# Expert stages whose list rows carry their token and weights, with six shared groups ahead of the list and list places of 256 and 128 rows

## The chip, the cores and the metric

The kernel runs on one core of one Trainium2 chip. The metric is the device time of one launch in microseconds (us). Three runs of the kernel before took 3293.65, 3300.22 and 3301.5 us, so the median is 3300.22. A separate execution was taken with the hardware profiler. It took 3303.56 us, and its span, from the first instruction to the last, is 3301.8 us. Every row shown below comes from that one execution. A profile names the engines PE (TensorE matmul), PEld (TensorE's weight load, which overlaps PE), DVE (VectorE), ACT (ScalarE), POOL (GpSimd) and SP (SyncE, whose queue issues most DMAs).

## The reference

The input `x` is 32 sequences of 128 tokens with 256 features, 4096 tokens in all. Six blocks are added to it one after another: a state space model, a cross attention, a transformer block with gated experts, a recurrence, a second cross attention, and a second expert block. The change touches the two expert blocks. The first of them, cut to what matters:

```
logits = h2 @ router_w                       # (4096, 8)
probs = softmax(logits); topw, topi = top_k(probs, 2); topw = softmax(topw)
combine = sum(one_hot(topi, 8) * topw[..., None], axis=1)
shared = (silu(h2 @ sh_gate) * (h2 @ sh_up)) @ sh_down
gate = einsum('td,edf->etf', h2, e_gate)
up = einsum('td,edf->etf', h2, e_up)
eout = einsum('etf,efd->etd', silu(gate) * up, e_down)
spec = einsum('etd,te->td', eout, combine)
return X + shared + spec
```

The width of an expert is 512. The second expert block has sigmoid scores, one up projection, no gate and no shared part. All arithmetic is in 32-bit floats.

## The kernel before

Tokens are worked on in 8 groups of 512 (`NG = 8`, `GT = 512`; a group is 4 tiles of 128 tokens, one per partition). The program is a run of stages. Each stage writes one instruction list per engine, by hand, in the order in which the functions are called, and engines meet at semaphores. No planner sets the order in the expert stages. At the end of a stage every engine drains and waits for the others (`pass_stage`, L2564). The stages `mamba`, `b`, `c` come ahead, then `d` (`experts`, from L1902), `r` with `e` behind it, and last `f` (`list_experts`, from L2412).

Stage `d` has four parts.

1. Each group's rows `H` are transposed and the router's logits are computed (L1693, L1978). Then VectorE alone picks the two experts of every token and gives each of the 8192 pairs of a token and an expert a row in a list in DRAM, sorted by expert (`router_vector`). The list is cut into places of 256 rows (`UR`), each of one expert. The number of rows per expert is known only on the chip, so 39 places are always worked on (`units_of_list`), whatever the counts are. In the end each place's expert is looked up (`expert_i`).
2. Four *shared* units (`SHN = NG // 2`), one per group: gate and up matmuls with 512 columns (L2229), silu on ScalarE (L2250), the product on VectorE (L2262), the down matmuls (L2187) and the add to `X` (L2279). Beside them VectorE copies a group's rows to a staging buffer (`stage_group`, L2093), and GpSimd sends them to the list with 64 indirect DMAs (L2118). There are two staging buffers. VectorE's copy for the next group waits until the DMAs of the buffer's last group have landed.
3. Thirty-nine *list* units. SP loads a place's rows (L2311) and its expert's weights into one of two buffers (L2318: gate and up, 1 MB, L2321: down, 0.5 MB). PE transposes the rows of the next place during a unit (L2214) and ScalarE copies them out of PSUM (L2239). The down matmuls of a unit are issued behind the next unit's first quarter (`f == 0`). VectorE copies their result to `y_rows` (L2281), and SP stores it to `out_by_expert` (L2325).
4. The other four shared units. GpSimd gathers, for each group, 8 tiles from `out_by_expert` (L2141). It has two buffers too. VectorE multiplies them by the pair's weights and adds them to `X` (`collect_group`, L2155), in pairs of groups between the products of the units.

Within a unit the quarter `f` on PE may start when the product of quarter `f - 2` is done (`after(pe, hidden, ...)`).

Stage `f` works on its own list in DRAM, `rows_in_place`, with a fixed region of 4096 rows per expert. It was filled during stage `e` with rows of 272 floats: 256 features, 8 weights and the token's number 8 times. Each of its 39 units loads a place (L2444) and weights into three buffers (L2447). VectorE reads weights and tokens out of the rows, scales the result (L2516), and GpSimd adds each tile of 128 rows to `out` in DRAM, by token, with an indirect DMA that accumulates (L2525). Two such DMAs may not overlap in the rows that they change, so GpSimd waits for a place's DMAs to land before it issues the next place's:

```
pl.wait_ge(mixed, UT * u + UT)
pl.wait_ge(sent_to, u + 1)
after(pl, added, 16 * UT * u)
```

The results `y` have two buffers. The table of places of stage `f` is computed by VectorE at the end of stage `e` (`ended_vector`, L848 to L863).

## Time and profile before

| what | value |
|---|---|
| time of the profiled execution, its span | 3303.56 us, 3301.8 us |
| median of three runs | 3300.22 us |
| busy share of the span | PE 84%, PEld 57%, DVE 58%, ACT 46%, POOL 44% |
| stage `d` from its first DMA to the next stage's first | 1409.56 to 2108.61 us |
| stage `f` from its first matmul to the end of the span | 2997.00 to 3301.8 us |
| HBM traffic | 154.17 MB read, 90.05 MB written, 74 GB/s over the span |

The page says which engines are busy overall. It mixes stages with different limits, so for a change in two stages a reader needs the same numbers for stretches of those stages, and then the instructions in order of time. "Idle before", in square brackets behind an instruction, is how long its engine did nothing just before it and what ended that. PE's clock in a stretch is the granted share of full speed. "x16" behind a row is the number of records it merges. Each float32 matmul of this program shows as two records, and a transpose as one.

### The profile page before, as it was taken

What the parts mean: (1) busy time and instruction counts of PE and PEld (TensorE: products, weight loads), DVE (VectorE), ACT (ScalarE), POOL (GpSimd) and SP (SyncE); (2) the same over time, 40 slices, a digit from 0 to 9 for tenths busy, and PEclk for the clock granted to TensorE, in tenths of its full rate; (3) what the DMA queues carried; (4) which work ended last, traced back from release to release, by engine and by line L of the source; (5) the groups of instructions that cost most, each with busy time, mean ns of one, the idle gap of its engine ahead of it and who ended that gap; (6) DMA issues with size and microseconds to landing.
All of it is one profiled execution on the core that took longest, in us unless ns stands there. A gap on an engine that the chain in (4) does not pass through costs nothing.

```text
span 3301.8 us, 49294 instructions
## 1 busy us (share of the span) xinstructions
PE 2775.8 (84%) x16680; PEld 1894.1 (57%) x16680; DVE 1904.4 (58%) x3429; ACT 1529.9 (46%) x2627; POOL 1460.3 (44%) x1559
## 2 busy tenths in 40 slices
PE   6888888867887888776999998699788888867998
PEld 2333333334555566533888885498455555546887
DVE  3878788875887688841222223500689888862111
ACT  4565556635675566510222221344566666642222
POOL 3666676654444577525000004500345555543444
PEclk8999999998998899988999999799899999988999
DMA  9600000000013000012566652200000100005775
GB/s 326 214 1 0 0 1 0 1 0 30 14 47 110 1 1 1 1 69 92 175 192 196 196 188 82 86 1 1 1 14 31 38 30 31 21 27 175 212 211 149
DMA packets 135984, 244.92 MB, mean 74 GB/s; under 512 B 16144, under 2 KB 107792, under 8 KB 125328
## 3 DMA queue, kind: packets, MB, share of 16 engines
q1 hardware_dynamic: 115344, 208.33, 19.4%
q0 software_dynamic: 20448, 34.11, 4.2%
q8 instruction: 110, 1.80, 0.2%
q14 instruction: 82, 0.67, 0.1%
HBM read 154.17 MB, written 90.05 MB: 74 GB/s over the span
## 4 chain that ended last, share of the span: by engine, by line
PE 34%; POOL 7%; DVE 6%; issue 6%; ACT 2%; POOLq 1%; another core or an unknown queue 1%; DMA 0%; SPq 0%; DVEq 0%; ACTq 0%
PE PS L2229 9%; PE PS L2187 5%; PE PS L1837 4%; PE PS L2476 4%; PE PS L2463 4%; POOL e_hs L1396 2%; POOL rows_by_expert L2118 2%; DVE e_mx L1299 1%; POOL e_qs L1399 1%; PE PS L1251 1%; POOL rows_in_place L831 1%; PE PS L1828 1%; PE PS L1194 1%; POOLq L2564 1%
## 5 line engine op out<-in xcount | busy, mean ns | idle before, releaser
L534 POOL TENSOR_TENSOR u_in<-dtx,b_rep 128x512 f32<-128x512 f32 x256 | 324.9, 1291 | 209.1 <-ACT b_rep L515 208.0
L550 DVE TENSOR_TENSOR_SCAN state<-PS,u_in 128x512 f32<-128x512 f32 x256 | 312.2, 1219 | 59.1 <-POOL u_in L534 34.9
L2250 ACT ACTIVATE d_act_b<-PS 128x256 f32<-128x256 f32 (+1 forms) x188 | 78.4, 419 | 511.7 <-PE PS L2229 432.7
L507 PE MATMUL PS<-scaled,ident 128*128 128x512 f32 x512 | 290.6, 651 | 28.6 <-DVE scaled L544 28.6
L2229 PE MATMUL PS<-d_unit_T,d_w 128*128 128x256 f32 x1248 | 284.0, 381 | 1.0 <-ACT d_unit_T L2239 1.0
L2262 DVE TENSOR_TENSOR d_hid<-d_act_b,PS 128x256 f32<-128x256 f32 (+1 forms) x188 | 87.3, 466 | 316.9 <-ACT d_act_b L2250 314.1
L1396 POOL TENSOR_TENSOR e_hs<-e_pr 128x512 f32<-128x512 f32 x128 | 162.6, 1270 | 229.3 <-ACT e_pr L1363 225.5
L2229 PEld LDWEIGHTS PS<-d_unit_T,d_w 128*128 128x128 f32 x1248 | 235.2, 191 | 32.0 <-issue 1.4
L523 ACT ACTIVATE PS<-dt,decay_rate 128x508 f32<-128x508 f32 x256 | 173.5, 686 | 132.0 <-DVE state L550 130.2
L544 DVE TENSOR_TENSOR scaled<-state,PS 128x512 f32<-128x512 f32 x256 | 169.4, 664 | 63.9 <-PE PS L488 52.2
L2136 POOL COPY d_slot_now<-d_slot 128x8 int32 x8 | 1.5, 194 | 461.1 <-DMA out_by_expert<-d_y_rows 443.3
L2525 POOL DMA_INDIRECT out<-f_y,f_token x78 | 121.1, 1553 | 185.0 <-DVE f_token L2509 117.8
L2187 PE MATMUL PS<-d_w,d_hid 128*128 128x256 f32 x880 | 198.0, 379 | 1.5 <-DVE d_hid L2262 1.5
L2187 PEld LDWEIGHTS PS<-d_w,d_hid 128*128 128x128 f32 x880 | 167.5, 190 | 28.2 <-issue 3.4
L1299 DVE TENSOR_REDUCE e_mx<-PS 128x8 f32<-128x1024 f32 x128 | 155.7, 1217 | 41.4 <-PE PS L1242 41.4
L1359 ACT ACTIVATE e_pT<-PS 128x1024 f32<-128x1024 f32 x128 | 130.7, 1021 | 96.2 <-PE PS L1251 96.2
L2516 DVE TENSOR_SCALAR f_y<-PS,f_share_rows 128x256 f32<-128x256 f32 x78 | 37.7, 483 | 235.1 <-PE PS L2463 220.8
L1251 PE MATMUL PS<-ident,e_pr 128*128 128x128 f32 x1024 | 144.7, 287 | 25.7 <-ACT e_pr L1363 25.3
L507 PEld LDWEIGHTS PS<-scaled,ident 128*128 128x128 f32 x512 | 96.4, 203 | 118.0 <-DVE scaled L544 86.0
L1837 PE MATMUL PS<-r_ring,r_wh 128*128 128x128 f32 x1024 | 161.3, 290 | 0.0
L1303 DVE TENSOR_TENSOR e_pr<-PS,e_mx 128x1024 f32<-128x1024 f32 x128 | 156.7, 1224 | 4.4
L1251 PEld LDWEIGHTS PS<-ident,e_pr 128*128 128x128 f32 x1024 | 122.0, 148 | 62.9 <-ACT e_pr L1363 55.0
(426 smaller groups left out, 6411.6 us busy)
## 6 DMA issues: line engine op xcount, KB each, us to landing
d_w<-in_d_w SPq DMA_DIRECT2D x41, 1024.0 KB, 4.9
f_w<-in_f_w SPq DMA_DIRECT2D x39, 1024.0 KB
rows_in_place<-blank SPq DMA_DIRECT2D x136, 272.0 KB, 4.5
d_w<-in_d_w SPq DMA_DIRECT2D x41, 512.0 KB, 3.9
f_unit_rows<-rows_in_place SPq DMA_DIRECT2D x39, 272.0 KB, 5.1
rows_by_expert<-zeros SPq DMA_DIRECT2D x39, 256.0 KB, 2.8
d_unit_rows<-rows_by_expert SPq DMA_DIRECT2D x39, 256.0 KB, 4.0
out_by_expert<-d_y_rows SPq DMA_DIRECT2D x39, 256.0 KB, 4.0
```

Source lines behind the costliest of these rows:

```text
L507: nc.tensor.matmul(YB[:, c], ident[:], scaled[:, (KD * n + c) % RC], start=False, stop=n == NS - 1).then_inc(m_y, 1)
L523: nc.scalar.activation(seqs(DECAY[:, k % RD])[:, :, 1:L], seqs(dt[:, p, c])[:, :, 1:L], ACT.Exp, scale=decay_rate[:, c * NS + n:c * NS + n ...
L534: nc.gpsimd.tensor_tensor(u_in[:, k % RU], dtx[:, p, c], b_rep[:, n % RB], ALU.mult).then_inc(m_u, 1)
L544: nc.vector.tensor_tensor(scaled[:, k % RC], state[:, k % 2], CB, ALU.mult).then_inc(m_hc, 1)
L550: nc.vector.tensor_tensor_scan(state[:, k % 2], DECAY[:, k % RD], u_in[:, k % RU], 0.0, ALU.mult, ALU.add).then_inc(m_h, 1)
L1251: step = nc.tensor.transpose(TR[:, m], pr[:, i % 2, m], ident[:])
L1299: nc.vector.tensor_reduce(mx[:, i % 2], scores_of(i), AX.X, ALU.max).then_inc(maxed, 1)
L1303: nc.vector.tensor_tensor(pr[:, i % 2], scores_of(i), mx[:, i % 2].unsqueeze(2).broadcast_to([128, MAPS, L]), ALU.subtract).then_inc(shift ...
L1396: nc.gpsimd.tensor_tensor(hs[:, i % 2], pr[:, i % 2, :, 0:L // 2], pr[:, i % 2, :, L // 2:L], ALU.add).then_inc(halved, 1)
L1837: product = nc.tensor.matmul(bank(at, m), wh_k[:, k, m * 128:m * 128 + 128], wide(ring[:, k, (at - 1) % (2 * WIN)]), start=False, stop=k = ...
L2187: step = nc.tensor.matmul(out_h[:, q], hid[:, p, f, row:row + 128], w_down[:, r, f], start=f == 0, stop=f == FC - 1)
L2229: step = nc.tensor.matmul(b, wt[:, r, c, f * 128:f * 128 + 128], x, start=c == 0, stop=c == KD - 1)
```

## The change

Stage `d` takes over what stage `f` does. The rows in `H` get 16 more floats: 8 with the token's weight for each expert and 8 with its number. They go to the list straight from `H`, with no staging copy. Unit results are scaled by VectorE and added by GpSimd, place by place, to a table by token in DRAM (`out_by_token`, zeroed in stage `b`). At the end SP loads that table in 8 pieces into four buffers, and VectorE adds it to `X`. Six shared units stand ahead of the list and two behind it.

Both expert stages get places of two sizes. There are 31 of 256 rows and 9 of 128 rows (71 tiles of 128 rows, where 39 places of 256 have 78). In stage `d` the order is one large place, nine times large, large, small, large, and three large ones. In stage `f` a small place stands behind every third or fourth large one. An expert's rows fill large places, and its last rows a small one where they fit. The tables are computed on VectorE with more and wider operations.

```
+def split_units(groups):
+    halves = (2 * groups * GT - 8) // 128 + 8
+    single = 8 + halves % 2
+    return (halves - single) // 2, single
+def unit_plan(groups):
+    full, single = split_units(groups)
+    kinds, done = [], 0
+    for n in range(full):
+        kinds.append((2, 2 * n))
+        if (n + 1) * single // full > done:
+            kinds.append((1, 2 * full + done))
+            done += 1
+    return kinds
+def slot_order(groups):
+    full, single = split_units(groups)
+    order = [(2, 0)]
+    for n in range(single):
+        order += [(2, 3 * n + 1), (2, 3 * n + 2), (1, n), (2, 3 * n + 3)]
+    return order + [(2, n) for n in range(3 * single + 1, full)]
+def half_of(groups):
+    full = split_units(groups)[0]
+    return [2 * n if kind == 2 else 2 * full + n for kind, n in slot_order(groups)]
...
-        SHN = NG // 2 if gated else 0
+        SHN = NG - 2
...
-            share_t = share.rearrange("p g s j -> p (g s) j")
-            for j in range(2):
-                link(V.tensor_copy(share_t[:, :, j], top[:, j]))
+            link(V.tensor_tensor(top[:, 4], top[:, 3], top[:, 2], ALU.subtract))
+            dve.sem_inc(routed, 1)
+            dve.wait_ge(exped, 2)
+            link(V.tensor_scalar(top[:, 0], top[:, 4], 1.0, None, ALU.add))
+            link(V.reciprocal(top[:, 0], top[:, 0]))
+            link(V.tensor_tensor(top[:, 1], top[:, 4], top[:, 0], ALU.mult))
+            link(V.tensor_tensor(lg[:], best[:, 0], by_e(top[:, 0]), ALU.mult))
+            link(V.tensor_tensor(tmp[:], best[:, 1], by_e(top[:, 1]), ALU.mult))
+            dve.wait_ge(marked, 2)
+            link(V.tensor_tensor(src_wide.rearrange("p g k d -> p (g k) d")[:, :, D:D + E], lg[:], tmp[:], ALU.add))
...
+            twice, single = units_e[:, E:], units_e[:, 0:E]
+            link(V.tensor_copy(count[:, 0], until[:, :, TILES - 1]))
+            link(V.tensor_scalar(count[:, 1], until[:, :, TILES - 1], -128.0, None, ALU.add))
+            link(V.tensor_tensor(filled[:], count.rearrange("p z e -> p (z e)").unsqueeze(2).broadcast_to([128, 2 * E, FILLS]),
+                                 whole.unsqueeze(1).broadcast_to([128, 2 * E, FILLS]), ALU.is_gt))
             link(V.tensor_reduce(units_e[:], filled[:], AX.X, ALU.add))
-            link(V.tensor_tensor_scan(last_e[:], ones_e[:], units_e[:], 0.0, ALU.mult, ALU.add))
-            link(V.tensor_tensor(base_e[:], last_e[:], units_e[:], ALU.subtract))
-            link(V.tensor_scalar(base_e[:], base_e[:], float(UR), None, ALU.mult))
+            link(V.tensor_tensor(starts[:, 1:E + 1], single, twice, ALU.subtract))
+            link(V.tensor_scalar(twice, twice, 2.0, None, ALU.mult))
+            link(V.tensor_tensor_scan(ends[:, 0:E], ones_e[:, 0:E], twice, 0.0, ALU.mult, ALU.add))
+            link(V.tensor_scalar(starts[:, 0:1], ends[:, E - 1:E], float(2 * FULL), None, ALU.max))
+            link(V.tensor_tensor_scan(ends[:, E:], ones_e[:], starts[:], 0.0, ALU.mult, ALU.add))
+            link(V.tensor_tensor(base_e[:, 0], ends[:, 0:E], twice, ALU.subtract))
+            link(V.scalar_tensor_tensor(out=base_e[:, 1], in0=ends[:, E + 1:], scalar=-1.0, in1=ends[:, 0:E], op0=ALU.add, op1=ALU.subtract))
+            link(V.tensor_copy(base_e[:, 2], twice))
+            link(V.tensor_scalar(base_e[:], base_e[:], 128.0, None, ALU.mult))
...
+            link(V.tensor_tensor(moved[:], place[:], over_n(2), ALU.is_ge))
+            link(V.tensor_tensor(moved[:], moved[:], over_n(1), ALU.mult))
+            link(V.tensor_tensor(place[:], place[:], over_n(0), ALU.add))
+            link(V.tensor_tensor(place[:], place[:], moved[:], ALU.add))
...
-        def stage_group(dve, turn, p):
-            g = 2 * turn + p
-            after(dve, in_list[p], 16 * 2 * GS * turn)
-            nc.vector.tensor_copy(staged_rows[:, p], rows_full[:, g])
-            nc.vector.tensor_copy(slot_now[:, p], slot[:, g]).then_inc(staged, 1)
...
         def to_list_pool(pl):
-            pl.wait_ge(listed, 16 * UNITS)
-            def group(turn, p):
...
+            for g in range(NG):
                 for k in range(GS):
                     for j in range(2):
                         nc.gpsimd.indirect_dma_start(
...
+                            rows_by_expert, bass.IndirectOffsetOnAxis(slot[:, g, k, j:j + 1], 0),
+                            src_wide[:, g, k], None).then_inc(in_list[g % 2], 16)
+        def to_tokens_pool(pl):
+            done = 0
+            for j in range(UNITS):
+                pl.wait_ge(taken, 2 * (j + SHN) + 4)
+                for k in range(tiles_at[j]):
+                    nc.gpsimd.indirect_dma_start(
+                        out_by_token, bass.IndirectOffsetOnAxis(token[:, j % 2, k:k + 1], 0), y_rows[:, j % 2, k], None,
+                        bounds_check=NG * GT - 1, oob_is_err=False, compute_op=ALU.add).then_inc(added, 16)
+                done += tiles_at[j]
+                pl.wait_ge(added, 16 * done)
+                pl.sem_inc(scattered, 1)
+        def note_vector(dve, j, jp, kind):
+            n = tiles_of[kind]
+            if isinstance(j, int):
+                dve.wait_ge(row_in[jp], 16 * (j // 2 + 1))
             else:
...
+                dve.wait_ge(row_in[jp], 8 * (j - jp) + 16)
+            nc.vector.tensor_tensor(mine_rows[:, jp, 0:n], unit_rows[:, jp, 0:n, D:D + E],
+                                    mine[:, j].unsqueeze(1).broadcast_to([128, n, E]), ALU.mult).then_inc(weighed, 1)
+            dve.wait_ge(scattered, j + 1)
+            nc.vector.tensor_copy(token[:, jp, 0:n], unit_rows[:, jp, 0:n, D + E]).then_inc(noted, 1)
+            dve.wait_ge(weighed, 2 * j + 1)
+            nc.vector.tensor_reduce(share_rows[:, jp, 0:n], mine_rows[:, jp, 0:n], AX.X, ALU.add).then_inc(weighed, 1)
+        def collect_group(dve, g):
+            dve.wait_ge(taken, 2 * (g + 2 + (UNITS if g >= SHN else 0)))
+            dve.wait_ge(got[g % GOT], 16 * (g // GOT + 1))
+            nc.vector.tensor_tensor(X[:, g], X[:, g], y_got[:, g % GOT], ALU.add).then_inc(combined, 1)
...
-                    step = nc.vector.tensor_copy(y_rows[:, p, h:h + 1], o)
-                step.then_inc(taken, 1)
+                    step = nc.vector.tensor_scalar(y_rows[:, p, h], o[:, 0], share_rows[:, p, h:h + 1], None, ALU.mult)
...
+            with eng.Fori(0, SINGLE) as turn:
+                j = 4 * turn + 1
                 unit(eng, j + SHN, *LST(j, 1), LST(j - 1, 0), "list")
-                unit(eng, j + (SHN + 1), *LST(j + 1, 0), LST(j, 1), "list")
-            unit(eng, SHN + UNITS - 2, *LST(UNITS - 2, 1), LST(UNITS - 3, 0), "list")
-            unit(eng, SHN + UNITS - 1, *LST(UNITS - 1, 0), LST(UNITS - 2, 1), None)
-            before = LST(UNITS - 1, 0)
-            for g in range(SHN, NG if SHN else 0):
-                now = SHR(g, 1 - g % 2)
-                unit(eng, UNITS + g, *now, before, None, again=g - SHN)
-                before = now
-            output(eng, (UNITS + NG if SHN else UNITS) - 1, *before)
-        def load_rows(sp, j, jp):
+                unit(eng, j + (SHN + 1), *LST(j + 1, 0), LST(j, 1), "half")
+                unit(eng, j + (SHN + 2), *LST(j + 2, 1, "half"), LST(j + 1, 0), "list")
+                unit(eng, j + (SHN + 3), *LST(j + 3, 0), LST(j + 2, 1, "half"), "list")
...
+        def load_rows(sp, j, jp, at, tiles):
             after(sp, turned, j - 1)
-            sp.dma_start(unit_rows[:, jp], list_units[:, j]).then_inc(row_in[jp], 16)
+            after(sp, weighed, 2 * j - 3)
+            after(sp, noted, j - 1)
+            sp.dma_start(unit_rows[:, jp, 0:tiles], list_rows[:, bass.ds(at, tiles)]).then_inc(row_in[jp], 16)
...
+            sp.wait_ge(scattered, UNITS + 2)
+            for g in range(NG):
+                after(sp, combined, g - GOT + 1)
+                sp.dma_start(y_got[:, g % GOT], out_rows[:, g]).then_inc(got[g % GOT], 16)
...
-        unit_of = rows_in_place.rearrange("(u r p) d -> p u r d", p=128, r=UT)
+        rows_at = rows_in_place.rearrange("(h p) d -> p h d", p=128)
+        tiles = [n for n, _ in unit_plan(NG)]
+        upto = [sum(tiles[:u]) for u in range(SLOTS + 1)]
+        late = lambda u: upto[max(u, 0)]
+        wide = lambda u: tiles[u] * 128```

GpSimd's instructions of stage `d` in their order before (`d_slot_now` is a copy of a group's list positions; the first DMAs scatter rows to the list, the last gather results):

```order
L2115 TENSOR_TENSOR d_mark<-eps 128x1
L2118 DMA rows_by_expert<-d_staged_rows,d_slot_now 9984x256 x8
...
L2136 COPY d_slot_now<-d_slot 128x8
L2138 TENSOR_TENSOR d_mark<-eps 128x1
L2141 DMA d_big<-out_by_expert,d_slot_now 128x256 x8
```

and now, the whole of the stage:

```order
L2425 MEMSET d_unit_no 128x1 x40
L2154 COPY H<-d_tokens 128x32x8
L2164 DMA rows_by_expert<-H,d_slot 9216x272 x64
L2173 DMA out_by_token<-d_y_rows,d_token 4096x256 x71
```

The scatters lost the waits between groups. The gathers are gone, and 71 DMAs that accumulate now run during the list.

PE in the loop over the list, one unit before (`d_unit_T` holds the place's rows, transposed):

```order
L2229 MATMUL PS<-d_unit_T,d_w 128x256 x4
...
L2187 MATMUL PS<-d_w,d_hid 128x256 x4
...
L2187 MATMUL PS<-d_w,d_hid 128x256 x4
L2229 MATMUL PS<-d_unit_T,d_w 128x256 x4
...
L2214 MATMUL PS<-ident,d_unit_rows 128x128 x4
```

and now the small unit of a turn, with the start of the large unit behind it:

```order
L2253 MATMUL PS<-d_unit_T,d_w 128x128 x4
...
L2209 MATMUL PS<-d_w,d_hid 128x256 x4
...
L2209 MATMUL PS<-d_w,d_hid 128x256 x4
L2253 MATMUL PS<-d_unit_T,d_w 128x128 x4
...
L2238 MATMUL PS<-ident,d_unit_rows 128x128 x4
...
L2253 MATMUL PS<-d_unit_T,d_w 128x256 x4
...
L2209 MATMUL PS<-d_w,d_hid 128x256 x4
L2253 MATMUL PS<-d_unit_T,d_w 128x256 x4
```

The small unit's own matmuls have half the columns, but the 8 down matmuls of the large place ahead of it stand inside it. Its own 4 stand in the large unit behind it.

VectorE at the seam between two list units, before:

```order
L2262 TENSOR_TENSOR d_hid<-d_act_b,PS 128x256
L2274 ISA
L2276 ISA
L2281 COPY d_y_rows<-PS 128x256
L2276 REGISTER_ALU
L2281 COPY d_y_rows<-PS 128x256
```

and now, from the last product of a unit to the first of the next (`d_token` holds a place's token numbers as integers):

```order
L2279 TENSOR_TENSOR d_hid<-d_act_b,PS 128x256
...
L2186 TENSOR_TENSOR d_mine_rows<-d_unit_rows,d_mine 128x16
L2188 REGISTER_ALU
L2189 CAST d_token<-d_unit_rows 128x2
L2190 ISA
L2191 TENSOR_REDUCE d_share_rows<-d_mine_rows 128x2
L31 ISA
L2278 ISA
L2279 TENSOR_TENSOR d_hid<-d_act_b,PS 128x256
```

Three instructions (`note_vector`) came in between. The cast waits until GpSimd's DMAs of the place two before have landed, and the next unit's first product is queued behind it.

## Rows read from the trace of the kernel before

**Rows 1.** Stretches: us, then busy us and records per engine, PE clock, DMA share, GB/s.

```profile
1451.00:1564.00 113.00, 84.55 (x230) 45.37 (x229) 27.41 (x58) 10.17 (x18) 63.96 (x72) 0.86 0.28 99
1564.00:1985.00 421.00, 421.00 (x2017) 370.43 (x2018) 97.56 (x230) 90.45 (x229) 0.00 (x0) 1.00 0.59 189
1985.00:2108.00 123.00, 95.59 (x297) 56.87 (x295) 46.03 (x102) 10.48 (x19) 64.62 (x80) 0.93 0.27 77
3000.00:3290.00 290.00, 288.46 (x1403) 252.17 (x1403) 51.64 (x194) 86.72 (x235) 118.02 (x76) 1.00 0.73 207
```

**Rows 2.** Chain that ended last: start us, length us, what; both lists.

```profile
1563.85 3.75 PE PS L2229 x8
...
1965.66 5.18 PE PS L2229 x24
...
1976.46 5.18 PE PS L2229 x24
...
3271.31 2.59 PE PS L2476 x12
...
3278.66 2.59 PE PS L2476 x12
```

**Rows 3.** Timeline, end of the list: start us, length us, engine, line, operation [idle before].

```profile
1974.34 0.42 DVE L2281 COPY d_y_rows<-PS 128x256 f32<-128x256 f32 x1 [1.23 <-PE PS L2187]
...
1980.02 0.38 ACT L2250 ACTIVATE d_act_b<-PS 128x256 f32<-128x256 f32 x1 [1.34 <-PE PS L2229]
1980.43 0.42 DVE L2262 TENSOR_TENSOR d_hid<-d_act_b,PS 128x256 f32<-128x256 f32 x1 [1.31 <-ACT d_act_b L2250]
...
1990.11 3.60 PE L2229 MATMUL PS<-d_xT,d_w 128*128 128x512 f32 x8
...
1997.00 13.90 PE L2229 MATMUL PS<-d_xT,d_w 128*128 128x512 f32 x32
```

**Rows 4.** Timeline of weight loads in the recurrence.

```profile
2161.17 0.30 PEld L1828 LDWEIGHTS PS<-r_xT,r_wi 128*128 128x128 f32 x2
2161.39 1.17 PEld L1837 LDWEIGHTS PS<-r_ring,r_wh 128*128 128x128 f32 x8
2162.48 0.30 PEld L1828 LDWEIGHTS PS<-r_xT,r_wi 128*128 128x128 f32 x2
```

**Rows 5.** Timeline, the router's end and the first product of the shared units.

```profile
1453.35 0.17 DVE L2064 TENSOR_TENSOR d_base_e<-d_last_e,d_units_e 128x8 f32<-128x8 f32 x1
...
1454.66 0.42 DVE L2068 TENSOR_TENSOR d_place<-d_place,d_base_e 128x256 f32<-128x256 f32 x1
...
1457.54 0.48 DVE L2074 TENSOR_TENSOR d_passed_e<-d_const,d_last_e 128x312 f32<-128x312 f32 x1
...
1459.79 0.68 DVE L2262 TENSOR_TENSOR d_hid<-d_act_b,PS 128x512 f32<-128x512 f32 x1
```

**Rows 6.** Timeline, the last group collected and the stage's end.

```profile
2104.46 3.38 DVE L2155 SCALAR_TENSOR_TENSOR X<-d_big,d_share_now,X 128x256 f32<-128x256 f32 x8 [4.99 <-DMA d_big<-out_by_expert,d_slot_now]
2108.61 0.35 SPq L1757 DMA_DIRECT2D r_wi<-in_r_wi  x1
```

**Rows 7.** Waits in stage f: engine, for whom: us in total, times, longest.

```profile
POOL out L2525 <- DVE f_token L2509: 117.8, 27, 24.2
POOL out L2525 <- DMA out<-f_y,f_token: 47.3, 10, 5.0
```

**Rows 8.** Timeline of stage f, a result on VectorE and the DMAs on GpSimd.

```profile
3059.33 1.55 POOL L2525 DMA_INDIRECT out<-f_y,f_token  x1 [4.96 <-DMA out<-f_y,f_token]
3061.18 1.55 POOL L2525 DMA_INDIRECT out<-f_y,f_token  x1 [0.30 <-issue]
3065.84 1.55 POOL L2525 DMA_INDIRECT out<-f_y,f_token  x1 [3.11 <-DVE f_token L2509]
...
3270.05 0.48 DVE L2516 TENSOR_SCALAR f_y<-PS,f_share_rows 128x256 f32<-128x256 f32 x1 [1.14 <-PE PS L2463]
...
3271.31 1.55 POOL L2525 DMA_INDIRECT out<-f_y,f_token  x1 [3.85 <-DVE f_token L2509]
```

517 lines of the change are left out of this document (241 added, 276 removed).

## The prediction

> **What bounds the kernel now.** I read the stretches first. Through the list of stage `d` PE is busy 421.00 of 421.00 us at the full clock, 2.4 GHz; in stage `f` it is busy 288.46 of 290. The four shared units ahead of the list keep it busy for only 84.55 of 113 us, the four behind it for 95.59 of 123 [rows 1]. So both lists cost what PE's instructions cost, and around the first list something else sets the time. The chain gives the unit: large places of `d` follow each other by 10.80 us, those of `f` by 7.35, and 24 records of 256 columns take 5.18 us, 0.216 each [rows 2]. A place of `d` is 48 such records (10.35 us) and 4 transposes (the other 0.45); one of `f` is 32 records (6.9) and 4 transposes. A record of 512 columns takes 13.90 / 32 = 0.43 us [rows 3].
>
> **Stage `d`, ahead of the list.** The router's chain on VectorE grows, and the first product waits behind it. A step costs 0.17 us at 8 elements, 0.42 at 256 and 0.48 at 312 [rows 5], so about 1 ns per element more, and 0.04 between steps. Added: three wide steps for the weights less two copies (+1.1), eight small ones and two widened for the counts (+1.8), three wide ones for the positions (+1.4), the wider table of places (+1.7, with two steps of 680 elements at 0.9). A staging copy less is -0.7, three small steps behind one tiny matmul at the stage's start about +0.5. Sum +5.8: the first product moves from 1459.79 to 1465.6 us and PE goes on at 1466.3. Then come 6 x 32 - 16 = 176 records of 512 columns (75.5 us) and 160 down records (34.5), and 2 us for a slower clock behind the gap (the granted mean of that stretch is 0.86 [rows 1]). That is 1578.4; 2.1 us of transposing and copying the first place, an estimate from its 4 transposes and two ScalarE copies, puts the first list matmul at 1580.5 instead of 1563.85 [rows 2]: **+16.7**. Two shared units of 20.6 us are in this. They are cheap because PE idled there: the scatters keep GpSimd busy for 64 of 113 us [rows 1] and have no staging to wait for now. They hide behind 112 us of PE.
>
> **The list.** Before: 1563.85 to 1990.11 [rows 2, 3], 426.3 us. After: 31 x 10.80 + 9 x 5.40 = 383.4, plus the down records of the last shared unit (6.9) less its own last ones (3.45): 386.9, so -39.4. This takes a small place at half price, which no row shows. From below: a load of the weights is hidden behind 256 columns now, and the nearest stream of small matmuls, the recurrence, starts loads 0.11 us apart (2161.17 to 2161.39, two loads), with ScalarE's waits 1.31 / 10 = 0.131 [rows 4]. Half price is 0.108. I take 0.115, the nearest row being 0.11: 288 records x 0.007 = +2.0. The upper end is 0.131 (+6.6), and if load and matmul did not overlap at all 0.214 (+30).
>
> The Trainium skill weighs against half price ("TensorE: Matmul & The Clock Gate", section "Back-to-back issue gap"): in a stream of loads and matmuls both set the spacing, and at 128 columns it gives 81 ns where a matmul alone is 56. By its 25 ns more per record this term would be 7.2 us instead of 2.0. The recurrence's 0.131 agrees with it, its 0.11 does not.
>
> Silu and product of a large place's last quarter end 0.94 us behind its matmuls (0.38 and 0.42 with hand-offs, 1980.02 to 1980.85 [rows 3]); a small place's quarter covers 0.86. With a hand-off to PE that is 0.15 nine times: +1.4.
>
> **The new wait.** VectorE may write a place's tokens only when GpSimd's DMAs of the place two before have landed, and the next product is queued behind it; PE waits for that product at its third quarter. No row of `d` shows such a landing, but stage `f` has the same DMAs. Call L the time from the end of the last issue to the next place's issue. Landing ended it 10 times, 47.3 us, longest 5.0 [rows 7], as 4.96 at 3059.33; three times of four VectorE ended it, so that L was shorter, 3.11 at 3065.84 [rows 8]. The mean over all is at most 7.35 - 3.4 = 3.95. An issue takes 1.55 and 0.30 between two, so 3.40 for a large place, and GpSimd starts 0.78 behind the result (3270.53 to 3271.31) [rows 8].
>
> Behind a small unit the room is least. It starts; 0.86 + 3.45 later the large place ahead is out, +0.5 for VectorE [rows 3], +0.8, +3.4, +L; the unit lasts 7.35; cast, reduction and product take 0.8. The product is there 2.45 + L into the large unit, and PE wants it at 5.64 (three quarters and transposes): a stall of L - 3.2, nine times. Between large units there is room up to L = 7.4. With L = 3.8: 9 x 0.6 = **+5.4** (L of 3.2: 0; of 5.0: +16). I take 3.8 because the mean was at most 3.95 and DMA gets busier by the ninth that the list gets shorter. List: -39.4 + 2.0 + 1.4 + 5.4 = **-30.6**.
>
> **Behind the list.** Before: 1990.11 to 2108.61 [rows 3, 6], 118.5 us, with waits of PE for products queued behind collecting; at the end VectorE waits 4.99 us for a gather [rows 6]. After: 64 records of 512 columns (27.5), 80 down records (17.25), the last add to `X` (1.7), two adds of 1024 elements (1.2 each by the rate above), 0.8 to the next stage: 49.7. The loads from the table can start 15 us in (3.4 + 3.5 + 0.5 + 0.8 + 3.4 + 3.8) and are wanted at 31, so they hide. **-68.8**. Stage `d` in all: 16.7 - 30.6 - 68.8 = **-82.7**.
>
> **Stage `f`.** PE's part falls from 39 x 7.35 = 286.7 to 35.5 x 7.35 = 260.9, -25.7. But a turn of three large and one small place is 25.7 us on PE and 3 x 3.40 + 1.55 + 4L = 11.75 + 4L on GpSimd. They meet at L = 3.5. With 3.8 GpSimd sets the pace: 1.2 us more, nine times, +10.8. PE's own small extras (1.0 and 1.4) hide under that. At the end the last, small place waits for the large one's landing: its issue comes 4.2 later, less 1.85 for the issue that is gone, +2.4. **-12.5** (L of 3.2: -21; of 5.0: +35). The longer table at the end of stage `e` (8 us instead of 5) runs beside its last scatters, and the other edits are small memsets on idle GpSimd: nothing.
>
> **Sum.** -82.7 - 12.5 = -95.2. Against the profiled execution, 3303.56, that is 3208.4. The median is 3.3 below it, so on its scale **3205 us**. For L above 3.9 the change as a whole is 50L - 286.
>
> **Rivals.**
> 1. *GpSimd keeps up* (L at most 3.5). For it: 3.11 at 3065.84, and 27 of the waits ended on VectorE [rows 7, 8]. Against: DMA share is 0.73 already [rows 1]. Stage `d` -86, `f` -22: 3192.
> 2. *Landing under load* (L of 4.3 to 5.7). For it: 4.96 happens now, with DMA at 0.73 [rows 1, 8]. Against: it happens once in four. With 5.0: -36, 3264.
> 3. *Slower than before*: the same wait with L over 5.7, from where 50L - 286 is positive. The small places then make GpSimd the limit of all of `f` and stall every turn of `d`. At 6.0: 3314. Against it: the longest wait now is 5.0 [rows 7], and the traffic grows by a ninth.
> 4. *Small places not at half price*: with 0.131 3210, with 0.214 about 3237. Against: the loads 0.11 apart [rows 4].
>
> The Trainium skill has a rule for the second and third ("DMA: Bandwidth & Descriptors", section "Latency and other measured facts"): access to HBM takes 0.2 us on average and 2 at high load. By it a landing of 3.1 could become 4.9, and the sum -41; the trace agrees that both lengths occur, 3.11 and 4.96.
>
> **How the numbers follow.** Forecast, L of 3.5 to 4.3: 0.55, by itself 3190 to 3230. Rival 1: 0.22. Rival 2: 0.12. Rival 3: 0.04. Rival 4 by more than 10 us: 0.07. Eight in ten lie between 3186 and 3245: below are only the fastest cases of rival 1, above are rival 3 and most of 2. A measurement of this kernel tells 0.3%, 10 us, from no change. Faster by more is all but rival 3 and the worst of rival 2: 0.95; within 0.3%: 0.01; slower: 0.04.
>
> **What would show it.** First list matmul near 1580 us; periods of 10.8 with 5.4 for a small unit; no wait of PE for products except one in four large units, below 1.5 us; 50 us from the last list matmul to the next stage; a turn of `f` of 26 to 27.5 us with GpSimd waiting for its own DMAs most of the time. The prediction is wrong if 128 columns cost over 0.13 us, if PE waits for weights in the lists, or if a place of `f` takes over 7.6 us.

## The result: slower by 1.2%, where 2.9% less was forecast

Before: 3300.86 us median of 4 runs (3293.65 to 3305.23). After: 3342.61 us median of 4 runs (3327.26 to 3345.07). The ratio is 1.0121, with a 95% interval of 1.0102 to 1.0140. The forecast was 3205 us, range 3186 to 3245: wrong, on the other side of no change. In the profiled executions the span goes from 3301.8 to 3342.3 us. Placed like the forecast's steps:

| stretch | before, us | after, us | forecast | measured | missed by |
|---|---|---|---|---|---|
| up to the first list matmul of `d` | 1563.85 | 1640.64 | +16.7 | +76.8 | 60.1 |
| list of `d` | 426.3 | 429.5 | -30.6 | +3.2 | 33.8 |
| behind the list, to the next stage | 118.5 | 49.8 | -68.8 | -68.8 | 0 |
| the rest, nearly all of it stage `f` | 1193.2 | 1222.5 | -12.5 | +29.3 | 41.8 |
| sum | | | -95.2 | +40.5 | 135.7 |

Later sessions ran on chips where the kernel before takes 3270 us and the one after about as much. That is a finding (below), and it explains most of the first row.

### The profile page after: what moved, and what is told of

Its sections match the earlier page's. It is cut to its first block, busy times and chain, and to the rows that moved or that the text cites. A ratio compares the mean times of both kernels' runs of the same rounds, so it can differ in the third digit from the quotient of the medians.

```text
span 3342.3 us, 49458 instructions
## 1 busy us (share of the span) xinstructions
PE 2745.0 (82%) x16590; PEld 1865.0 (56%) x16590; DVE 1899.3 (57%) x3490; ACT 1520.8 (46%) x2639; POOL 1496.7 (45%) x1618
## 4 chain that ended last, share of the span: by engine, by line
PE 26%; DMA 8%; POOL 7%; issue 6%; DVE 6%; ACT 2%; another core or an unknown queue 2%; POOLq 0%; DVEq 0%; SPq 0%; ACTq 0%
PE PS L2253 9%; DMA out<-f_y,f_token 6%; PE PS L2209 5%; PE PS L1892 4%; POOL e_hs L1451 2%; DMA out_by_token<-d_y_rows,d_token 2%; POOL out L2559 1%; POOL e_qs L1454 1%; DVE e_mx L1354 1%; PE PS L1306 1%; POOL rows_in_place L872 1%; PE PS L1883 1%; PE PS L1249 1%; PE PS L2496 1%
## 5 line engine op out<-in xcount | busy, mean ns | idle before, releaser
L2270 ACT ACTIVATE d_act_b<-PS 128x256 f32<-128x256 f32 (+2 forms) x192 | 76.5, 399 | 547.1 <-PE PS L2253 467.0
L2173 POOL DMA_INDIRECT out_by_token<-d_y_rows,d_token x71 | 110.2, 1553 | 427.0 <-DVE d_y_rows L2300 401.9
L2253 PE MATMUL PS<-d_unit_T,d_w 128*128 128x256 f32 (+1 forms) x1280 | 268.3, 363 | 29.2 <-DVE d_hid L2279 28.1
L2253 PEld LDWEIGHTS PS<-d_unit_T,d_w 128*128 128x128 f32 x1280 | 225.6, 194 | 58.7 <-DVE d_hid L2279 31.5
L2279 DVE TENSOR_TENSOR d_hid<-d_act_b,PS 128x256 f32<-128x256 f32 (+2 forms) x192 | 84.3, 440 | 288.4 <-ACT d_act_b L2270 233.7
L2559 POOL DMA_INDIRECT out<-f_y,f_token x71 | 110.6, 1557 | 224.8 <-DVE f_y L2550 167.1
L2209 PE MATMUL PS<-d_w,d_hid 128*128 128x256 f32 x824 | 186.7, 380 | 2.5 <-DVE d_hid L2279 1.5
L2550 DVE TENSOR_SCALAR f_y<-PS,f_share_rows 128x256 f32<-128x256 f32 x71 | 32.9, 482 | 264.8 <-DMA out<-f_y,f_token 188.6
L2209 PEld LDWEIGHTS PS<-d_w,d_hid 128*128 128x128 f32 x824 | 155.7, 190 | 28.8 <-issue 6.1
L2253 PE MATMUL PS<-d_xT,d_w 128*128 128x512 f32 (+1 forms) x256 | 120.9, 631 | 60.4 <-issue 49.6
L2496 PE MATMUL PS<-f_w,f_hid 128*128 128x256 f32 x568 | 146.1, 414 | 27.3 <-DVE f_y L2550 26.7
L2530 ACT ACTIVATE f_hid<-PS 128x256 f32<-128x256 f32 (+1 forms) x160 | 57.5, 360 | 227.8 <-PE PS L2509 226.8
```

The source lines that it names most:

```text
L2209: step = nc.tensor.matmul(out_h[:, q], hid[:, p, f, row:row + 128], w_down[:, r, f], start=f == 0, stop=f == FC - 1)
L2253: step = nc.tensor.matmul(b, wt[:, r, c, f * 128:f * 128 + 128], x, start=c == 0, stop=c == KD - 1)
L2496: step = nc.tensor.matmul(DB(r), hid[:, u % 2, f, r * 128:r * 128 + 128], w_down[:, u % RING, f], start=f == 0, stop=f == FC - 1)
L2559: nc.gpsimd.indirect_dma_start(tokens_of, bass.IndirectOffsetOnAxis(token[:, u % RING, k:k + 1], 0), y[:, u % 2, k], None, bounds_check=NG ...
```

## The profile after

The stretches of the kernel after, with columns as in [rows 1]: beside the list scatters, the shared units behind them, the list, and stage `f`.

```profile
1459.00:1554.00 95.00, 35.11 (x85) 17.49 (x83) 12.19 (x24) 3.89 (x7) 61.64 (x64) 0.69 0.32 116
1554.00:1651.00 97.00, 95.31 (x308) 58.82 (x309) 19.60 (x32) 10.85 (x20) 0.00 (x0) 0.98 0.03 12
1651.00:2068.00 417.00, 387.90 (x1948) 340.71 (x1947) 106.54 (x343) 86.14 (x235) 105.59 (x68) 0.98 0.68 190
3030.00:3320.00 290.00, 263.09 (x1252) 227.06 (x1251) 44.45 (x177) 74.09 (x223) 101.45 (x66) 0.94 0.68 192
```

PE no longer fills the list or stage `f`, as it did in [rows 1]. Beside the scatters it is busy for 35 of 95 us.

The chain that ended last shows both losses of stage `d` and the table's marks; it answers to [rows 2]. Columns: start us, length us, what.

```profile
1478.54 2.04 issue
1480.62 61.92 another core or an unknown queue
1542.61 10.46 another core or an unknown queue
1553.72 0.70 DVE d_hid L2279
...
1640.64 1.96 PE PS L2253 x8
...
1662.48 5.18 PE PS L2253 x24
...
1673.06 4.35 PE PS L2253 x24
1677.52 3.73 PE PS L2209 x16
1682.54 1.55 POOL out_by_token L2173
1684.39 7.85 DMA out_by_token<-d_y_rows,d_token
1693.11 5.45 PE PS L2253 x24
...
1726.09 8.11 DMA out_by_token<-d_y_rows,d_token
1735.08 7.13 PE PS L2253 x24
...
2064.91 8.61 PE PS L2253 x32
...
2119.84 1.42 DVE r_st L1819 x4
```

The list starts at 1640.64 us. The piece at 2064.91 is 24 records of the last place and 8 of the first shared unit, which begins 24 x 0.216 later, at 2070.09. The next stage starts at 2119.84.

**The stop.** From 1480.6 to 1553 us nothing that the profile knows holds the chain. ScalarE's timeline there (start us, length us, operation [idle before <- releaser]):

```profile
1480.58 0.60 ACT L2270 ACTIVATE d_act_b<-PS 128x512 f32<-128x512 f32 x1 [2.78 <-issue]
1542.56 0.60 ACT L2270 ACTIVATE d_act_b<-PS 128x512 f32<-128x512 f32 x1 [61.39 <-remote]
1553.09 1.08 ACT L2270 ACTIVATE d_act_b<-PS 128x512 f32<-128x512 f32 x2 [9.93 <-remote]
```

VectorE has one such wait too:

```profile
1488.72 0.69 DVE L2298 TENSOR_TENSOR X<-X,PS 128x512 f32 x1 [6.82 <-PE PS L2209]
1520.28 0.69 DVE L2298 TENSOR_TENSOR X<-X,PS 128x512 f32 x1 [30.88 <-remote]
```

By the profile PE had delivered by 1494.3. ScalarE's code between 1480.58 and 1542.56 is the wait for PE's second quarter and no other operation. Both operations belong to the first pass of the loop over shared units, and no branch stands between them: the first unit's four operations end with the one at 1477.21, and 1480.58 is the first inside the loop. VectorE's wait stands between the two halves of one result.

The trace also records when a semaphore rises, which no view shows. PE's matmuls of that second quarter end at 1490.88 (ends of matmuls are modelled), and their semaphore rose at 1542.54, 0.02 us before ScalarE went on. The two halves of the down matmuls end at 1484.00 and 1487.45, and their semaphore rose at 1488.58 and 1520.14, the second one just ahead of VectorE. In a_after (below) the same three distances are 0.02 us or less. In the kernel after the semaphores that ScalarE and VectorE raise were in time beside the scatters. So both engines waited for PE's semaphores.

GpSimd sends its 64 list scatters all the while, the last one here:

```profile
1543.47 0.96 POOL L2164 DMA_INDIRECT rows_by_expert<-H,d_slot  x1 [0.30 <-issue]
```

The kernel before had shorter stops of this kind. Of its trace, ScalarE and then GpSimd:

```profile
1494.45 0.60 ACT L2250 ACTIVATE d_act_b<-PS 128x512 f32<-128x512 f32 x1 [22.66 <-remote]
```

```profile
1490.87 0.96 POOL L2118 DMA_INDIRECT rows_by_expert<-d_staged_rows,d_slot_now  x1 [0.30 <-issue]
1496.53 0.19 POOL L2115 TENSOR_TENSOR d_mark<-eps 128x1 f32<-128x1 f32 x1 [4.71 <-DVE d_slot_now L2094]
```

Its wait of 22.66 us ends in a pause of GpSimd. That kernel sent its scatters in rows of 24, 16, 16 and 8 here. In b_before (below), where nothing stopped, the same code sent all 64 with no pause over 0.6 us. So the pauses came from the stops themselves: VectorE's staging copy, which GpSimd waits for, was late.

**The new wait in `d`.** Waits from 1652 to 2068 us of the kernel after (us in total, times, longest):

```profile
DVE d_token L2189 <- POOLq L2178: 78.7, 32, 8.2
PE PS L2253 <- DVE d_hid L2279: 28.1, 9, 3.9
```

PE waits nine times, once for each small place. The scatter rows sent at 1684.39 took 7.85 us; the median of all 71 is 3.9. SP's timeline shows what stands beside them: 512 KB, 1 MB and again 512 KB of weights within 7 us, since a small place needs as much weight as a large one.

```profile
1681.40 0.33 SPq L2343 DMA_DIRECT2D d_w<-in_d_w  x1
1682.09 0.38 SPq L2333 DMA_DIRECT2D d_unit_rows<-rows_by_expert  x1
1684.52 0.33 SPq L2340 DMA_DIRECT2D d_w<-in_d_w  x1
1688.11 0.33 SPq L2343 DMA_DIRECT2D d_w<-in_d_w  x1
```

**Stage `f`.** Waits from 3030 to 3320 us; they answer to [rows 7].

```profile
DVE f_y L2550 <- DMA out<-f_y,f_token: 185.3, 28, 11.5
POOL out L2559 <- DVE f_y L2550: 164.1, 33, 7.7
PE PS L2496 <- DVE f_y L2550: 26.7, 7, 5.3
```

Before, GpSimd mostly waited for VectorE's tokens, that is for PE's pace, and VectorE waited for PE. Now VectorE waits for scatters to land. The chain is scatter, landing, next scatter, with 0.86 us from the landing to the next issue, in which GpSimd turns to the next place and VectorE writes a result:

```profile
3110.66 1.56 POOL out L2559
3112.53 6.09 DMA out<-f_y,f_token
3119.48 1.56 POOL out L2559
3121.34 8.44 DMA out<-f_y,f_token
```

From issue to landing a scatter of `f` takes 2.7 / 5.1 / 8.4 us (shortest, median, longest).

## Experiments on the stop

**Both kernels again.** First on what chip: in the first session and in the one of e11 and e12 the kernel before takes 3300 us, in the other five about 3270. (The expectations speak of "the second chip"; they mean the numbers of the sessions without the stop.)

> The changed kernel itself once more, for a chip on which the four variants of it ran without the stop beside the list scatters (TensorE busy 80 of 80 us from 1480 to 1560, against 54.66 in the kernel before and less in the changed kernel on the first chip). If the stop belongs to the chip or its state and not to what the variants changed: about 3273 us where the kernel before takes 3272, ratio 1.000, and no wait of ScalarE over 15 us from 1480 to 1560. If it belongs to the changed kernel's code (both a pause and a straight piece of code, and also the shifted code of the other two variants, took it away): ratio 1.012 again, with the wait of 61 us.

> The kernel before once more, for its profile on this chip. Stop belongs to the chip: TensorE is busy over 75 of 80 us from 1480 to 1560 (54.66 on the first chip) where its four shared units have work, and the span is some 28 us shorter, about 3273. Otherwise as before: 3302 and waits of ScalarE of 39 us there.

Measured: a_after 3278.06 us against 3272.53, ratio 1.0022 (1.0007 to 1.0037); b_before 3269.59. No engine waits for "remote" in either. From 1455 to 1575 us of a_after, where the kernel after on the first chip was stopped:

```profile
1455.00:1575.00 120.00, 114.05 (x339) 65.32 (x338) 29.02 (x48) 13.14 (x22) 61.64 (x64) 0.97 0.26 92
```

The first list place's copy is at 1576.8 us and the first list matmul at 1577.8. The forecast of 1580.5 for it holds where nothing stops. The forecast of +16.7 does not, since the kernel before is earlier there too. Its first list matmul is at 1547.97, behind transposes that wait for the last scatters to land:

```profile
1545.83 1.12 PE L2214 MATMUL PS<-ident,d_unit_rows 128*128 128x128 f32 x4 [19.82 <-DMA d_unit_rows<-rows_by_expert]
```

These 19.8 us are what the longer front could fill there. From b_before to a_after the first copy moves by +29.9 us, the list takes +2.7, the part behind it -51.0, the stages between +5.3 and `f` +22.6: together the +9.5 of the two spans. Where b_before was expected to keep PE busy for over 75 of 80 us, it was busy for 59: those four shared units are over before 1530. Both kernels' stops belong to the chip or to something else of the session; which, the runs don't tell.

**A pause** (e1, and alone once more as e13) and **no loop** (e2, again as e14):

```
                if g:
                    pl.wait_ge(in_list[(g - 1) % 2], 16 * 2 * GS * ((g - 1) // 2 + 1))
```

```
-            with eng.Fori(0, SHN // 2 - 1) as pair:
+            for pair in range(SHN // 2 - 1):
```

> Changed kernel, but GpSimd waits after every 8 of the 64 list scatters until they have landed. Held-fetch theory: in the changed kernel ScalarE, VectorE and TensorE come to code that they must fetch while GpSimd sends scatters without a pause, and the fetch gets through only in a pause (ScalarE's product waits 61.4 us from 1481 to 1542.6, beside the last of 64 scatters). Then the shared units go on in the first pause, 10 to 13 us after they stop; the list scatters end some 20 us later (about 1565) and TensorE's idle time beside them falls from about 70 us to 15 to 30: about 3300 us (3290 to 3315). Rival: what stops the engines needs the whole list to be sent, or is the traffic itself: then the later end of the scatters makes it worse, 3345 to 3365.

> Changed kernel, but the four shared units behind the first stand one after the other in the code and not in a loop. Held-fetch theory with the loop's jump as the cause: what an engine has already fetched in line lasts it for some units, so that at least ScalarE (some 15 instructions a unit) is not held; the 61 us wait of ScalarE goes or is much shorter, 3275 to 3320 us. Held-fetch theory without the loop as the cause (any engine that reaches the end of what it holds is held, loop or not): TensorE, with over 100 instructions a unit, is held in its place, 3320 to 3345. Rival (the stop has nothing to do with code): no change, 3335 to 3350.

> The changed kernel with the pause after every 8 list scatters, once more. On a chip with the stop (the kernel before at 3300): held theory, 3342 - 65 = 3277 us, ratio 0.993, since e12 against e11 gave 54 us for the pause and the changed kernel's own stop is 62 us longer than on the other chip. Rival (the pause helped only with e12's other edits): 3330 to 3345. On a chip without it: 3276 where the kernel before is at 3272.

Measured on chips without the stop: e1 3276.19 us, ratio 1.0010 (0.9993 to 1.0027), again 1.0001 (0.9985 to 1.0016); e2 1.0008 (0.9993 to 1.0024), again 1.0007 (0.9989 to 1.0024). I first took e1 and e2 as support for the theory, 66 us under 3342. The kernel before, 29 us lower in the same session, showed that they said nothing.

**The pause on a chip that stops.** e11 and e12 differ by the pause alone (both have also four buffers in `d` and the small places last in `f`).

> As the run before it (nine small places last), with the pause after every 8 list scatters. On a chip without the stop: the same time within 5 us. On a chip with the stop (the kernel before at 3301 and not 3272): held-fetch theory, 30 to 60 us less than the run before it, and no wait of ScalarE over 15 us beside the scatters; rival (the stop needs no unbroken row of scatters): the same or up to 20 us more.

Measured, with the kernel before at 3299.84: e11 3259.85 us, ratio 0.9882 (0.9865 to 0.9898); e12 3205.44, ratio 0.9703 (0.9682 to 0.9723). So the pause is worth 54 us there. First e11 beside its scatters, then e12:

```profile
1447.00:1555.00 108.00, 48.24 (x126) 26.32 (x125) 14.46 (x26) 4.67 (x8) 61.87 (x64) 0.70 0.28 103
```

```profile
1455.00:1575.00 120.00, 114.04 (x341) 65.34 (x340) 27.42 (x44) 13.49 (x23) 61.59 (x64) 0.97 0.26 92
```

ScalarE of e11 stops at the same place in its code, and goes on while GpSimd still sends (until 1530.9):

```profile
1467.72 0.60 ACT L2272 ACTIVATE d_act_b<-PS 128x512 f32<-128x512 f32 x1 [2.78 <-issue]
1521.84 0.60 ACT L2272 ACTIVATE d_act_b<-PS 128x512 f32<-128x512 f32 x1 [53.52 <-issue]
```

In e12 a pause of GpSimd is as short as this, and ScalarE passes the same place at 1485.16 with its usual wait of 9.74 us:

```profile
1479.89 0.96 POOL L2168 DMA_INDIRECT rows_by_expert<-H,d_slot  x1 [0.30 <-issue]
1482.58 0.96 POOL L2168 DMA_INDIRECT rows_by_expert<-H,d_slot  x1 [1.73 <-DMA rows_by_expert<-H,d_slot]
```

Shown, by e11 and e12 where the kernel before takes 3300 us: beside an unbroken row of 64 scatters the engines stop, and waiting for every 8 to land removes it. Shown too: ScalarE and VectorE wait for semaphores of PE that rise late. Not shown: whether PE finished late or only its signal was late, and by what way the scatters do it. My theory, that the engines lack code, does not fit. No long wait begins at a branch. Of the two instruction queues that the profile records, the one named q8 brought a packet of 16 KB at 1484.6 us in a_after. In the kernel after on the first chip it came at 1556.1, 13.5 us after ScalarE had gone on, so it did not end that wait. The Trainium skill ("Runtime: NRT & Kernel Launch", section "Instruction fetch mechanics") says that a taken branch whose target isn't held makes the engine wait for a fetch by DMA; ScalarE's wait of 61.39 us stands behind no branch, so the traces do not agree with this rule as its cause.

**A gap without a landing** (e15, and e16 in place of e12's pause) was to tell whether any gap does:

```
+                    nc.gpsimd.memset(big[:, 0:2048], 0.0).then_inc(numbered, 1)
+                    pl.wait_ge(numbered, g + 2)
```

> The changed kernel, where GpSimd sets 2048 numbers of an unused tile to zero after every 8 list scatters (some 1.8 us, by 6.9 us for 8192 in the trace of the changed kernel) and does not wait for the scatters to land. On a chip with the stop: if any gap between the scatters ends it, 3275 to 3290 as with the pause; if the scatters that were sent must have landed, 3330 or more. On a chip without it: 3273 to 3278.

> e12 with the gap of e15 in place of the wait for landing. On a chip with the stop (the kernel before at 3300): if any gap ends it, 3205 us as e12, ratio 0.970; if the scatters must have landed, 3245 to 3260 as e11, ratio 0.988. On a chip without it (3272): 3205 us, ratio 0.980, 10 us under the version with 256 rows alone (3215).

Both sessions had no stop: e15 ratio 1.0002 (0.9985 to 1.0018), e16 3205.37 us, ratio 0.9796 (0.9774 to 0.9819). Open: whether any gap does, and whether code without a loop would help, as e2 and e14 never met the stop.

## Experiments on the list of `d`

**Places of 256 rows alone in `d`** (e4): 39 of them; the count for small places is

```
-link(V.tensor_scalar(count[:, 1], until[:, :, TILES - 1], -128.0, None, ALU.add))
+link(V.tensor_scalar(count[:, 1], until[:, :, TILES - 1], 0.0, None, ALU.add))
```

and the loops run over large places only.

> Changed kernel, but the first expert stage has 39 places of 256 rows, the last keeps small ones. Theory: the small places of the first stage save 5.4 us each of TensorE and lose 4 to 6 us each to the wait for the scatters of the place before, which land after 7.5 to 8.8 us beside the weights of two places: 39 x 10.80 = 421 us against 417 us in the changed kernel, so 3342 + 4 = 3346 us (3338 to 3354), and no scatter takes over 6 us to land in that stage. By my forecast's step (small places worth 30.6 us): 3373. Rival: the long landings are there without small places too: over 3373, as each place would then wait.

Measured: 3265.52 us, ratio 0.9981 (0.9968 to 0.9995), 0.4% under a_after's. From the first to the last copy of a place's rows e4's list takes 412.0 us, a_after's 417.8: nine small places in place of eight large ones lose 6 us (5 to 9, since nine other executions of this list took 416.8 to 421.2). The theory had them win 4. Scatters land after 2.7 / 3.8 / 4.7 us here, and after 2.7 / 3.8 / 8.8 with small places, so the long landings belong to these.

**Four buffers of results and tokens in `d`** (e5):

```
-        y_rows = t("y_rows", [128, 2, UT, D])
+        y_rows = t("y_rows", [128, 4, UT, D])
```

(`token` likewise.)

> Changed kernel, but the first expert stage has four buffers of result rows and of tokens and not two, so that VectorE waits for the scatters of the fourth place back. Theory: the nine turns with a small place take 41.7 to 44.3 us and not 37.8 because VectorE's copy of the tokens waits up to 8.2 us for the place before; with four buffers this wait goes, the stage is 31 to 42 us shorter, 1 to 1.3% under the changed kernel on the same chip (3235 where that takes 3273), and the copy waits under 5 us in all. Rival: the wait only moves, to TensorE waiting for weights (1.5 MB in 5.4 us) or to slower clocks: under 15 us shorter.

Measured: 3230.48 us, ratio 0.9875 (0.9851 to 0.9900), 48 us under a_after. The list takes 379.9 us, 37.9 less. Landings are as long (3.3 / 3.9 / 9.3), but only GpSimd waits for them, from 1585 to 1970 us:

```profile
POOL out_by_token L2181 <- DMA out_by_token<-d_y_rows,d_token: 74.0, 11, 8.6
```

The list is 35.1 us shorter than that of the kernel before in the same session (415.0). The forecast without its new wait was -39.4 + 2.0 + 1.4 = -36.0.

## Experiments on stage `f`

Its length from the first copy of a place's rows to the end of the span, and landing from issue (shortest / median / longest):

| kernel | `f`, us | landing, us |
|---|---|---|
| before, first session; b_before | 298.4; 298.8 | 2.7 / 4.6 / 6.3 (b_before) |
| after, first session | 327.5 | 2.7 / 5.1 / 8.4 |
| a_after | 321.4 | 2.7 / 4.8 / 8.1 |
| e3, 256 rows alone | 298.8 | 2.7 / 4.8 / 6.6 |
| e7, no adding | 277.6 | 2.1 / 4.4 / 5.8 |
| e8, half the weights | 295.4 | 2.7 / 4.7 / 7.2 |
| e9, four result buffers | 355.5 | 2.7 / 6.8 / 8.8 |
| e12, small places last | 288.0 | 2.7 / 4.8 / 7.5 |

Seven other executions that leave this stage as in the kernel after took 314.4 to 323.4 us, so a difference of a few us from a_after is not read here.

**256 rows alone** (e3: `full, single = units_of_list(groups), 0` in `unit_plan`):

> Changed kernel, but the last expert stage has 39 places of 256 rows again, the first keeps 31 and 9 small ones. Theory: in the last stage the small places bring the next 1 MB of weights into half the time, the accumulating scatters beside them land after 5 to 8 us in place of 4, and as GpSimd sends a place's scatters only when the last place's have landed, it sets the time: without small places the stage takes the 297 us that it took before instead of 324, so 3342 - 27 = 3315 us (3308 to 3322). Rival: landings are late for another reason (the whole list is later, other state of the memory): 3335 to 3345. By my forecast's step the small places were worth 12.5 us: 3355.

Measured: 3254.33 us, ratio 0.9943 (0.9924 to 0.9962), 24 us under a_after. The stage is as long as before. So the small places cost 22.6 us in `f` by these two profiles.

**No adding** (e7: `compute_op=ALU.add` taken out), **half the weights** (e8: `w[:, r, 0:UPS]` only from the fourth place on):

> Changed kernel, but the scatters of the last expert stage write their rows instead of adding them (the sum of a token's two rows is left out). On the second chip the changed kernel's last stage takes 321 us from its first rows to the end of the span where the kernel before takes 299, and a scatter lands after 2.7 / 4.8 / 8.1 us (shortest, median, longest). If the adding itself makes the landing long: median under 3.8 and the stage at 285 to 300 us. If it is the load of the queues (1 MB of weights a place): median 4.5 or more, and the stage at 315 to 322.

> Changed kernel, but from the fourth place of the last expert stage only the first half of each place's weights (512 KB of 1 MB) is loaded, and the second products use the weights of earlier places. If the weights beside them make the scatters land late: median under 4.0 us, longest under 6, and the stage (321 us in the changed kernel on the second chip) at 290 us or less, since TensorE alone needs 25.7 us for three large places and a small one. If it is the adding itself: landing as before, 4.8, and the stage over 312 us.

Measured: e7 3231.21 us (0.9861 to 0.9906 of before), e8 3254.18 (0.9936 to 0.9969). e7's stage is under my range, but its median landing is over it: the gain is in the issue. Of e7, then of a_after (ns shortest / median / longest):

```profile
L2559 POOL DMA_INDIRECT out<-f_y,f_token x71: 984/985/998, 2961.6 to 3219.2; - x71
```

```profile
L2559 POOL DMA_INDIRECT out<-f_y,f_token x71: 1553/1557/1603, 2967.6 to 3270.7; - x71
```

71 issues shorter by 0.572 us are 40.6 us of GpSimd's row, and the stage is 43.8 shorter. In e8 the median hardly moves and the stage gives back 26.0 us. GpSimd's idle time between two places falls from a mean of 4.62 us to 3.97, which makes 26 us over 40 places: the weights make the long landings, not the usual ones. Both theories of these two runs hold in part. GpSimd sets the stage's pace with issue and landing.

**Four result buffers** (e9: `y` with four, the wait for `late(u - 3)`):

> Changed kernel, but with four buffers of result rows in the last expert stage in place of two. GpSimd sends a place's scatters only when those of the place before have landed, whatever the buffers. Theory: GpSimd's turn of three large places and a small one (11.75 us and four landings of 4.8, 31 us) is longer than TensorE's 25.7 us and sets the stage: no more than 5 us gained (ratio to the kernel before on the same chip 1.001 to 1.002 still). Rival: only the uneven landings stop TensorE (up to 8.1 us, median 4.8) and more buffers even them out, as in the first expert stage: 15 to 25 us gained, ratio 0.995 to 0.997.

Measured: 3312.98 us, ratio 1.0127 (1.0095 to 1.0158): 35 us slower than a_after. Neither theory has it. A typical place of e9, by SP and then by GpSimd:

```profile
3091.54 0.38 SPq L2477 DMA_DIRECT2D f_unit_rows<-rows_in_place  x1
3092.68 0.33 SPq L2480 DMA_DIRECT2D f_w<-in_f_w  x1
```

```profile
3091.41 1.55 POOL L2559 DMA_INDIRECT out<-f_y,f_token  x1 [7.37 <-DVE f_y L2550]
3093.27 1.56 POOL L2559 DMA_INDIRECT out<-f_y,f_token  x1 [0.30 <-issue]
```

The tokens still have three buffers, and their copy stands ahead of the result in VectorE's order. It now waits for the landing in nearly every place (185.3 us, 24 times, from 2990 to 3240). SP's load of rows waits for that copy, and the weights are behind it. So each landing starts both the next scatters and 1.3 MB of loads, and the scatters land after 6.8 us. PE waits for weights as well (31.2 us, 18 times). This reading of one profile was not tested by a run of its own, for which the tokens would have to get four buffers as well.

**Small places last** (e11, e12: `[(2, 2 * n) for n in range(full)] + [(1, 2 * full + n) for n in range(single)]`):

> Four buffers in the first expert stage, and in the last one the nine places of 128 rows behind the 31 of 256, not among them. If GpSimd's turn (2.45 us and a landing of 4.8 for a large place, 0.6 us and a landing for a small one) or TensorE (7.35 us for a large place), whichever is longer, sets the stage place by place: 31 x 7.35 + 9 x 5.4 = 276 us in place of 39 x 7.35 = 287, so 10 us under the version with 256 rows alone (3215 on the second chip, ratio 0.984): 3205 there, ratio 0.981. If the landings get longer beside 1 MB of weights every 5.4 us (6 to 8 us): the nine take 60 to 77 us and the version is equal or up to 18 us over, ratio 0.984 to 0.989. If mixing was not the matter: the stage takes 320 us as in the changed kernel, ratio 0.990.

Measured: the stage takes 287.2 us in e11 and 288.0 in e12, 11 less than with 256 rows alone, as expected; the ratio of e11 is that of a chip that stops (above).

**Versions that beat both kernels.** e6 (four buffers in `d`, 256 rows alone in `f`):

> Four buffers in the first expert stage, and 39 places of 256 rows in the last one (small places in the first alone). If the two act by themselves: 31 to 42 us and 19 us off the changed kernel (the 256-row places alone gave 3273 - 19 = 3254 on the second chip), about 3215 us there, 1.5 to 2% under the kernel before. If the wait only moves: about 3240 to 3250.

> Four buffers in the first expert stage, 39 places of 256 rows in the last, and the pause after every 8 list scatters. On a chip that doesn't stop beside the list scatters: as without the pause, ratio 0.984 to the kernel before (within 0.002), since the pauses only delay the list's end from 1543 to about 1565 and the first place of the list starts at 1575. On a chip that stops (the first one), held-fetch theory: the stop ends in the first pause, and the ratio is 0.975 or less, since the kernel before has its own stops there; rival there: the stop stays at 60 to 70 us, ratio 0.99.

Measured: 3215.29 us, ratio 0.9838 (0.9814 to 0.9862); with the pause (e10) 3215.69, ratio 0.9829 (0.9808 to 0.9850). The two parts act by themselves. Best are e12, 0.9703 where the chip stops, and e16, 0.9796 where it doesn't: 3205 us on both.

## Why the prediction was wrong

**"They hide behind 112 us of PE."** Failed on the first chip: +60.1 of the miss. PE's idle time in [rows 1] (busy 84.55 of 113 us) was put down to staging and priced as time that the change fills. A part of it was stops of ScalarE and VectorE, which waited for PE's late semaphores beside GpSimd's scatters. The stops ended in pauses of the scatters, for which GpSimd waited for a staging copy. With the staging gone the row was unbroken, and the stop grew. On a chip without it PE is busy as forecast (114.05 of 120 us), but the step still costs +29.9 and not +16.7: the kernel before has only 19.8 us of idle time ahead of its list there, and the shared units and the router's chain add 47 us of work.

**The list, -30.6.** Half price for a small place nearly holds, with the extras that were forecast: e5 gives -35.1 against -36.0, and its turns of three large places and a small one take 38.4 us, so a small one 6.0 (5.8 by the forecast's terms). What failed is the wait's size. L - 3.2 has the right place and number (nine, one per small place), but L was 3.8 there and is about 6.3: 7.85 us from the issue's start to landing, less 1.55 for the issue. Nine times 3.1 are 27.9; PE's waits sum to 28.1 where +5.4 was forecast. The other 11 us come largely behind these waits, where PE is slower at first (24 records in 7.13 us at 1735.08 instead of 5.18). The mean granted clock is 0.98 instead of 1.00, by my estimate some 8 us over the 417 us of the list. The forecast had no term for them; e5 gives both back at once, 37.9 us.

**L was taken as a mean of evenly spaced places.** Landings were bounded by `f`'s pace of before. A small place halves the time in which the next weights must come, so the traffic is dense just where the room is least. "DMA gets busier by the ninth that the list gets shorter" is the sentence that failed.

**Behind the list, -68.8.** Right to 0.1 us, 49.8 against 49.7, on the first chip. In b_before the part from the last place's copy on is 17.6 us shorter than on the first chip, where VectorE waited 23.6 us for "remote" beside the gathers, and the gain is 51.0.

**Stage `f`, -12.5.** The mechanism, that GpSimd's turn of 11.75 + 4L replaces PE's 25.7, was right, and without the adding's longer issue the stage comes near PE's own 298.4 - 25.7 = 272.7 us (e7: 277.6). By the forecast's own sum, which comes to 41L - 169 for this stage, the measured +29.1 is an L of 4.8 in the first session, and the +22.6 of a_after one of 4.7, not 3.8. Read from GpSimd's timeline, the mean idle time between two places is 4.70 and 4.62 us; before it was 3.92. This is rival 2's range of L. The sum 50L - 286 is -46 for 4.8, as the stop and the denser weights of `d` were not in it.

**Rivals.** Rival 1 fell. Rival 4 fell (small places are near half price). Rival 3 has the sign and its places, but its turning point, L over 5.7 everywhere, was not needed: beyond the forecast the front alone brought 60 us. The chance of 0.95 for faster came from one question, L, with the front taken as certain.

## What to carry to other kernels

An idle engine beside a stream of DMAs is not free time until the rows say what holds it: a wait for "remote" or "an unknown queue" is a finding, not a remainder. Price a new wait with the traffic of the moment in which it stands, not with a mean; where a step gets shorter but its loads don't, that moment is the dense one. Where an engine sends long rows of indirect DMAs, a short wait for the last few to land cost nothing here (e13: ratio 1.0001) and took the stop away in the one session that had it.

## What the runs showed of the hardware

- The same program on the same data stops for some 70 us beside 64 unbroken scatters in one session and not at all in another. What comes late is PE's semaphores, by up to 52 us. Waiting after every 8 scatters for their landing removed the stop of e11 (54 us).
- An adding scatter of 128 rows of 1 KB costs GpSimd 1.557 us, a plain one 0.985, and from 3020 to 3220 us the adding ones of a_after took 147 DMA packets each, the plain ones of e7 47.
- More buffers can cost: they moved `f`'s wait to an instruction that starts the loads, and the landing went from 4.8 to 6.8 us.
